# The field pairs of layer 0 in six tiles and a remainder of 35 pairs, instead of seven tiles

## What is computed

```python
x0 = xk = inputs                      # (512, 39, 16)
for idx, (W, b) in enumerate(params): # W: (39, fk, 128)
    z = jnp.einsum('bhd,bkd,hks->bsd', x0, xk, W) + b[None, :, None]
    z = jax.nn.relu(z)
    if idx != n_layers - 1:
        xk = z[:, :64, :]; direct.append(z[:, 64:, :])
    else:
        direct.append(z)
logit = jnp.sum(jnp.concatenate(direct, axis=1), axis=-1)
```

## Time and profile before

| | |
|---|---|
| time, median of 3 runs | 683.54 us (683.5 to 683.76) |
| the profiled execution's own time, span | 687.57 us, 685.8 us |
| busy: PE, DVE, POOL, ACT | 633.7 (92%), 587.2 (86%), 315.5 (46%), 252.4 us (37%) |
| L647, f32 matmuls of the whole groups | x928, 434.5 us busy |
| L637, L638, L639, split groups | x256 each, 143.5, 101.5, 101.2 us |
| L582 and L574, products | x253 and x128 |
| DMA | 129.97 MB, mean 190 GB/s |

### The profile page before, as it was taken

The page is one execution under the profiler, slowest core; times in us unless marked ns, Lnnn a source line. Parts: engine busy times, 40 slices in busy tenths (PEclk is TensorE's granted clock), DMA queues, the critical chain, the costliest instruction groups (busy, mean ns, idle before and its releaser), DMA issues.

```text
span 685.8 us, 5970 instructions
## 1 busy us (share of the span) xinstructions
PE 633.7 (92%) x1856; PEld 347.2 (51%) x1856; DVE 587.2 (86%) x548; ACT 252.4 (37%) x330; POOL 315.5 (46%) x391
## 2 busy tenths in 40 slices
PE   0169798979999999999999999999999999999998
PEld 0025354535555555555555555555555555555544
DVE  2049798968999999999999999999999999999920
ACT  2013335324434434343344443443434444333312
POOL 6752764746546453636464454635473131322210
PEclk9979999989999999999999999999999999999999
DMA  9689818864765849394857567584939474260100
GB/s 209 172 268 359 246 42 291 247 238 127 227 222 158 298 126 328 61 332 94 293 155 249 191 188 267 148 305 90 349 59 327 111 260 170 86 220 1 63 0 1
DMA packets 125630, 129.97 MB, mean 190 GB/s; under 512 B 59646, under 2 KB 67598, under 8 KB 125599
## 3 DMA queue, kind: packets, MB, share of 16 engines
q1 hardware_dynamic: 117679, 128.16, 57.6%
q0 software_dynamic: 5120, 1.32, 2.1%
q10 hardware_dynamic: 2800, 0.12, 0.3%
HBM read 123.18 MB, written 6.39 MB: 189 GB/s over the span
## 4 chain that ended last, share of the span: by engine, by line
PE 79%; ACT 0%; issue 0%
PE z L647 50%; PE z L637 8%; PE z L638 7%; PE z L639 7%; PE z L654 1%; PE z L711 1%; PE z L655 1%; PE top L701 1%; PE z L701 0%; PE tp L701 0%; PE top L694 0%; PE xk L717 0%; PE tp L628 0%; PE tp L630 0%; PE z L694 0%; PE tp L694 0%
## 5 line engine op out<-in xcount | busy, mean ns | idle before, releaser
L647 PE MATMUL z<-whole,w 128*128 128x512 f32 (+2 forms) x928 | 434.5, 601 | 17.0 <-DVE whole L582 16.2
L647 PEld LDWEIGHTS z<-whole,w 128*128 128x128 f32 (+2 forms) x928 | 177.5, 193 | 176.6 <-issue 156.7
L582 DVE TENSOR_TENSOR whole<-bc,xk 128x1024 f32<-128x1024 f32 (+1 forms) x208 | 231.3, 1131 | 28.6 <-PE z L647 19.5
L421 ACT ACTIVATE high<-raw 128x1024 fp32r<-128x1024 f32 (+1 forms) x128 | 135.3, 1058 | 293.4 <-DVE raw L574 238.6
L320 POOL DMA_INDIRECT emb<-in_tables,rows_all x160 | 169.7, 1060 | 54.4 <-issue 53.6
L558 DVE TENSOR_TENSOR low<-raw,high 128x1024 fp32r<-128x1024 f32 (+1 forms) x128 | 161.7, 1263 | 7.9 <-issue 4.6
L637 PE MATMUL z<-high,w_high 128*128 128x512 f32 (+1 forms) x256 | 143.5, 561 | 9.7 <-issue 5.6
L574 DVE TENSOR_TENSOR raw<-bc,xk 128x1024 f32<-128x1024 f32 x112 | 135.8, 1212 | 0.0
L338 POOL TENSOR_TENSOR stack<-stack_raw,stack 64x512 fp32r<-64x512 f32 x32 | 45.0, 1406 | 196.9 <-ACT stack L428 196.8
L638 PE MATMUL z<-high,w_low 128*128 128x512 f32 (+1 forms) x256 | 101.5, 397 | 0.0
L639 PE MATMUL z<-low,w_high 128*128 128x512 f32 (+1 forms) x256 | 101.2, 395 | 0.0
(11 more groups left out here) (55 smaller groups left out, 179.2 us busy)
## 6 DMA issues: line engine op xcount, KB each, us to landing
bc<-fields SPq DMA_DIRECT2D x64, 1024.0 KB, 5.9
rot<-fields SPq DMA_DIRECT2D x16, 1280.0 KB
bc<-fields SPq DMA_DIRECT2D x16, 768.0 KB
rot<-fields SPq DMA_DIRECT2D x16, 512.0 KB
fields<-xt SPq DMA_DIRECT2D x64, 80.0 KB
bc<-fields SPq DMA_DIRECT2D x32, 128.0 KB
rep<-fields SPq DMA_DIRECT2D x48, 80.0 KB
emb<-in_tables,rows_all POOLq DMA_INDIRECT x160
```

Source lines behind the costliest of these rows:

```text
L421: act.activation(high[0:m, k % PART_SLOTS], raw[0:m, k % RAW_SLOTS], ACT.Copy).then_inc(high_ready, 1)
L582: nc.vector.tensor_tensor(whole[0:rows, n % WHOLE_SLOTS, 0:len(tiles)], left, right, ALU.mult).then_inc(whole_ready, 1)
L647: ins = nc.tensor.matmul(z[layer][:, :], w[layer][0:m, WHOLE_AT[layer, t], :], whole[0:m, k % WHOLE_SLOTS, u], start=(t == 0), stop=(layer ...
```

## The change

Layer 0 has six tiles of 128 rows: `left0` now holds the fields in four runs with different rotations, chosen so that with the six right windows RIGHT0 the 768 rows meet 745 of the 780 pairs (a repeated pair has weight 0). The 35 pairs left over are loaded three times, into 105 rows of `rest`, left and right factor, with 12 DMAs. Their product goes through `stack_raw` and `stack`: ACT copies all 105 rows, rows 64 to 98 become the low part, and the weights (high or low per row, in an additional slot of `w_high`) are laid out so that one fp32r pass does what the split groups do in three. Layer 0 has three groups, the second split.

The low part is subtracted by the DVE for chunks 0 to 2 and by GpSimd from chunk 3 on, between the fold of layer 2 and the stack of (1, p + 1). The pass itself is put into the next step's groups: behind the second group for chunks 1 and 2, behind the eighth (g = 7, layer 1 of chunk c - 1) from chunk 3 on, and at the end of layer 0 in chunk 0. `layer0_out` waits for it. All stacks, those of layer 0 too, have numbers in STACK_NO. Weight preparation has a few more small operations. The diff, cut (slices of ROWS0 rows that become all 128 are left out, and so are the weight preparation and the host's layout):

```diff
-ROT = FIELDS // 2 + 1
-ROT_PER_TILE = PART // FIELDS
-T0 = -(-ROT // ROT_PER_TILE)
-TURN = FIELDS + 1
-ROWS0 = ROT_PER_TILE * TURN
-LAST0 = (ROT - (T0 - 1) * ROT_PER_TILE) * TURN
+RUNS0 = ((0, 6), (FIELDS, 10), (2 * FIELDS, 37), (3 * FIELDS, 0))
+RIGHT0 = (10, 11, 12, 13, 28, 29)
+T0 = len(RIGHT0)
+REST = ((11, 11, 17), (11, 10, 18))
+REST_ROWS = sum(length for _, _, length in REST)
+COPIES = 3
+REST_ALL = slice(0, COPIES * REST_ROWS)
+REST_LOW = slice(KEEP, KEEP + REST_ROWS)
...
+REST_BY_VECTOR = 3
+REST_AFTER = (1, 7)
...
+def left0_field(p):
+    return (p + [distance for first, distance in RUNS0 if first <= p][-1]) % FIELDS
...
-        STACK_NO = {x: n for n, x in enumerate(x for x in STEPS if x[0])}
+        STACK_NO = {x: n for n, x in enumerate(STEPS)}
+        REST_BEHIND = {STEPS[n + 1]: x[1] for n, x in enumerate(STEPS[:-1]) if x[0] == 0 and x[1]}
...
         def layer0_read(engine, c):
...
+            engine.wait_ge(stack_ready, STACK_NO[0, c] + 1)
+        def load_rest(queue, c):
+            for copy in range(COPIES):
+                row = copy * REST_ROWS
+                for field, distance, length in REST:
+                    for side, first in enumerate((field, field + distance)):
+                        src = bass.AP(fields.tensor, c * CHUNK_ROWS + first * N, [[N, length], [1, N]])
+                        queue.dma_start(rest[row:row + length, side, :], src).then_inc(rest_in, 16)
+                    row += length
...
-                for r in range(ROT_PER_TILE):
-                    src = bass.AP(fields.tensor, at, [[N, TURN], [1, N]])
-                    sp.dma_start(rep[r * TURN:(r + 1) * TURN, :], src).then_inc(rep_in, 16)
+                for (first, distance), (end, _) in zip(RUNS0, RUNS0[1:] + ((PART, 0),)):
+                    src = bass.AP(fields.tensor, at + (first + distance) % FIELDS * N, [[N, end - first], [1, N]])
+                    sp.dma_start(rep[first:end, :], src).then_inc(rep_in, 16)
                 if c > 1:
                     layer0_read(sp, c - 1)
-                for first, last, arrived in ((0, GT, rot_first), (GT, T0, rot_rest)):
-                    src = bass.AP(fields.tensor, at + first * ROT_PER_TILE * N, [[N, PART], [ROT_PER_TILE * N, last - first], [1, N]])
-                    sp.dma_start(rot[:, first:last, :], src).then_inc(arrived, 16)
+                for t in range(0, T0, GT):
+                    src = bass.AP(fields.tensor, at + RIGHT0[t] * N, [[N, PART], [(RIGHT0[t + 1] - RIGHT0[t]) * N, GT], [1, N]])
+                    sp.dma_start(rot[:, t:t + GT, :], src).then_inc(rot_rest if t else rot_first, 16)
+                if c:
+                    load_rest(sp, c)
...
             def stack_part(layer, c):
+                n, lower = STACK_NO[layer, c], slice(KEEP, PART) if layer else REST_LOW
                 own_done()
-                pool.wait_ge(stack_high, STACK_NO[layer, c] + 1)
-                pool.tensor_tensor(stack[KEEP:PART, :], stack_raw[KEEP:PART, :], stack[KEEP:PART, :], ALU.subtract).then_inc(stack_low, 1)
-                issued["stacks"] += 1
+                pool.wait_ge(stack_high, n + 1)
+                pool.tensor_tensor(stack[lower, :], stack_raw[lower, :], stack[lower, :], ALU.subtract).then_inc(stack_low, 1)
+                issued["stacks"] = n + 1
...
                 fold(2, p - 1)
+                if p + 2 in IN:
+                    stack_part(0, p + 2)
                 if p + 1 in IN:
                     stack_part(1, p + 1)
...
-                n = STACK_NO[layer, c]
+                n, filled = STACK_NO[layer, c], slice(0, PART) if layer else REST_ALL
                 act.wait_ge(stack_ready, n + 1)
                 if n:
                     act.wait_ge(stack_free, n)
-                act.activation(stack[:, :], stack_raw[:, :], ACT.Copy).then_inc(stack_high, 1)
+                act.activation(stack[filled, :], stack_raw[filled, :], ACT.Copy).then_inc(stack_high, 1)
...
-                act.wait_ge(whole_free, wholes_to(0, c, G0 - 1))
+                act.wait_ge(stack_free, STACK_NO[0, c] + 1)
...
+            act.wait_ge(stored, 16 * STORES)
+            load_rest(act, 0)
             for g in SPLIT[0]:
                 high_part(0, 0, g)
+            turned(1)
+            stack_part(0, 0)
             layer0_out(0)
...
             turned(2)
             for g in SPLIT[0]:
                 high_part(0, 1, g)
+            stack_part(0, 1)
             layer0_out(1)
...
                 layer2_out(p - 1)
+                if p + 2 in IN:
+                    stack_part(0, p + 2)
...
-                        dve.wait_ge(rot_rest, (c + 1) * 16)
+                        dve.wait_ge(rot_rest, (c + 1) * 16 * (G0 - 1))
                     tiles = tiles_of(0, g)
-                    m = LAST0 if T0 - 1 in tiles else ROWS0
-                    product(0, c, g, rot[0:m, tiles[0]:tiles[-1] + 1, :], left[0:m, None, :].to_broadcast([m, len(tiles), N]))
+                    product(0, c, g, rot[:, tiles[0]:tiles[-1] + 1, :], left[:, None, :].to_broadcast([PART, len(tiles), N]))
                     lows(LAG)
+                n = STACK_NO[0, c]
+                if n:
+                    dve.wait_ge(stack_low, n)
+                dve.wait_ge(rest_in, (c + 1) * 16 * COPIES * len(REST) * 2)
+                nc.vector.tensor_tensor(stack_raw[REST_ALL, :], rest[:, 0, :], rest[:, 1, :], ALU.mult).then_inc(stack_ready, 1)
+                lows(LAG)
+                if c == 0:
+                    rest_low(0)
+            def rest_low(c):
+                n = STACK_NO[0, c]
+                dve.wait_ge(stack_high, n + 1)
+                nc.vector.tensor_tensor(stack[REST_LOW, :], stack_raw[REST_LOW, :], stack[REST_LOW, :], ALU.subtract).then_inc(stack_low, 1)
...
+                    if g == 0 and (layer, c) in REST_BEHIND and REST_BEHIND[layer, c] < REST_BY_VECTOR:
+                        rest_low(REST_BEHIND[layer, c])
...
-                    m = LAST0 if layer == 0 and t == T0 - 1 else ROWS[layer]
-                    ins = nc.tensor.matmul(z[layer][:, :], w[layer][0:m, WHOLE_AT[layer, t], :], whole[0:m, k % WHOLE_SLOTS, u],
-                                           start=(t == 0), stop=(layer == 0 and t == T0 - 1))
+                    ins = nc.tensor.matmul(z[layer][:, :], w[layer][:, WHOLE_AT[layer, t], :], whole[:, k % WHOLE_SLOTS, u],
+                                           start=(t == 0), stop=False)
...
+            def rest_of(c):
+                pe.wait_ge(stack_low, STACK_NO[0, c] + 1)
+                nc.tensor.matmul(z[0][:, :], w_high[REST_ALL, PARTS, :], stack[REST_ALL, :], start=False, stop=True).then_inc(stack_free, 1)
...
+                    if (layer, c) in REST_BEHIND:
+                        other = REST_BEHIND[layer, c]
+                        if g == REST_AFTER[other >= REST_BY_VECTOR]:
+                            rest_of(other)
                 if layer:
                     stacked(layer, c)
+                elif c == 0:
+                    rest_of(0)
```

More of the change, by code:

```diff
@@ L85, in tower @@
         w = [sb(f"w{n}", [PART, W[n], OUT]) for n in range(3)]
[L86 to L87 removed]
+        w_high = sb("w_high", [PART, PARTS + 1, OUT], fp32r)
+        w_low = sb("w_low", [PART, PARTS + 1, OUT], fp32r)
         wt3 = sb("wt3", [PART, H2 // PART])
@@ L99, in tower @@
         rot = sb("rot", [PART, T0, N])
-        rep = sb("rep", [ROWS0, N])
+        rest = sb("rest", [COPIES * REST_ROWS, 2, N])
+        rep = sb("rep", [PART, N])
         bc = [sb(f"bc{n}", [PART, T1, N]) for n in range(2)]
@@ L118, in tower @@
         to_split = rows[:, 0:PARTS, :]
-        w0_rev = rows[:, PARTS:PARTS + T0, :]
+        w0_rev = rows[:, PARTS:PARTS + T0 + 2, :]
+        rest_w = rows[:, PARTS + T0 + 2:PARTS + T0 + 4, :]
         wt1 = bc[0][:, 0:2, :]
@@ L132, in tower @@
         top = [bank(f"top{n}") for n in range(2)]
-        left0 = top[1][0:ROWS0, :]
+        left0 = top[1][:, :]
         h1_banks = (top[0], top[1], tp, z[0])
@@ L416, in high_part @@
             def high_part(layer, c, g):
-                k, m = SPLIT_NO[layer, c, g], ROWS[layer]
+                k = SPLIT_NO[layer, c, g]
                 act.wait_ge(raw_ready, k + 1)
@@ L555, in low_part @@
             def low_part(layer, c, g):
-                k, m = SPLIT_NO[layer, c, g], ROWS[layer]
+                k = SPLIT_NO[layer, c, g]
                 dve.wait_ge(high_ready, k + 1)
-                nc.vector.tensor_tensor(low[0:m, k % PART_SLOTS], raw[0:m, k % RAW_SLOTS], high[0:m, k % PART_SLOTS], ALU.subtract).then_inc(low_ready, 1)
+                nc.vector.tensor_tensor(low[:, k % PART_SLOTS], raw[:, k % RAW_SLOTS], high[:, k % PART_SLOTS], ALU.subtract).then_inc(low_ready, 1)
             def lows(age):
@@ L567, in product @@
             def product(layer, c, g, left, right):
-                m = ROWS[layer]
                 if g in SPLIT[layer]:
@@ L580, in product @@
                     tiles = tiles_of(layer, g)
```

(36 more changed lines are left out.)

55 lines of the change are left out of this document (31 added, 24 removed).

## The result

The changed kernel takes **734.13 us** (median of 4 runs, 732.11 to 736.15) against 683.52 for the kernel before on the same chip: ratio **1.0727** (95% interval 1.0689 to 1.0765), 50.6 us slower. The forecast was 701.3 with a range up to 714. The time is close to the 736 of another rival, the landing in the burst; that is a coincidence, since the landing waits were 0.5 us a cycle longer than forecast and not 3.5.

What follows compares the result with a forecast made beforehand. TensorE was taken as the bound at 37.37 us a cycle, the DVE close behind. +4.4 through p = 1 (including +1.2 at the start), +14.6 for ten cycles, -1.1 and 0.1 at the end: +17.8, median 701.3, range 677 to 714.

Steps and rivals of the forecast that it cites:

- the landing in the burst: Rival: in the cycles, gathers land among the `rep` and `rot` loads, +3.5 for ten cycles, 736; chance 0.18, shared with very late rows.
- The bound: Steady cycle: TensorE never idles in 37.37 us, the DVE could do 36.4; after the change TensorE needs 36.6 without waits.
- the passes: TensorE, per chunk: one f32 tile (0.86) goes and one fp32r pass (0.233) comes, -0.62 a cycle.
- the products: DVE, per chunk: an 80x512 product goes and a 105x512 one comes, 0.60 either way, so 0.
- (a): Up to the third chunk: `z[0]` emptied later, TensorE's wait at (2, 0) about 4; net +1.2, between -1 and +5.
- (b): At p = 1: the DVE's product waits for the rest subtraction after a late landing; next stack product at 159.8, +4.4.
- a rival of their own: The 35 rows arrive late: 17-row loads use one engine, chunks 0 and 3 wait, +5, 706; much too late shares chance 0.18.
- the rule: Loads of the rest: a DMA uses the largest engine count up to 16 dividing its rows, so 17 rows use one.
- (c): Ten cycles with gathers, p = 2 to 11: the DVE waits on GpSimd, 39.0 a cycle against 37.37, +14.6.
- the fold's collision: End of GpSimd's chain: the fold falls into the DVE's third subtraction, begins at 20.44 and takes 2.0, to 22.44.
- (d): p = 12 and 13, a rest but no gathers: TensorE bounds, 36.9 and 36.75 against 37.37 twice, -1.1.
- The rival of the Trainium skill's SBUF page: GpSimd's gathers start on time despite DVE subtractions, the DVE hardly waits, cycles about 36.85 to 36.9, 679.6; chance 0.20.

Runs made afterwards that it cites:

- the last version: The changed kernel with 18-row pieces, a separate stack for the rest, and ACT serving layer 2's first split group before emptying `z[0]` of chunk 1: 676.17 us, ratio 0.9905.
- with full loads: The changed kernel with all pieces of the rest at 18 rows instead of 17 and 18, its wait on GpSimd kept: 714.09 us, ratio 1.0445.

## Why the prediction missed

**The bound, the passes, the products: right.** TensorE's 36.6 us a cycle were an inference from start-to-start times; the last version runs at it. The DVE's subtractions of layer 1 stood where the forecast had laid them: at 12.53, 15.93 and 19.33 in the cycle shown.

**(a) and (b), the start: wrong, by 20.4 of 24.8 us.** The forecast was 159.8 for the first stack product of layer 2 behind p = 1; 180.20 was measured. The step that failed is the place of the rest's DMAs in the sum. It stood there as twelve issues on SP at 0 cost, with the data spread over 16 engines, 1.3 us; the loads through one engine were put in a rival of their own, whose price was +5, in chunks 0 and 3 only. The runs show 22.6 us in four chunks, and 20.0 or 23.9 for the pieces of 17 rows alone. Two things went wrong in it. I took the steady cycle's slack of 20 us as the rule and looked at the start for two chunks, though in chunks 2 and 3 the last of the twelve loads is issued (106.45 and 136.63) only 2.7 and 2.1 us before the DVE wants the rows (109.18 and 138.71). In chunks 0 and 1 the DVE wants them 10.1 and 7.9 us behind the last issue, about the 9.1 that the slow loads alone take, and waits 6.24 and 2.54; other transfers ran beside them there, at 258 to 377 GB/s from 30 to 40 us, and what part of the wait is theirs was not separated. And I gave the rule little because no row bore it out, where no row spoke against it either. The other half of (a) was right: the wait at (2, 0) forecast at about 4 was 4.60,

```profile
93.91 0.79 PE L701 MATMUL z<-high,w_high 128*128 128x512 f32 x1 [4.60 <-DVE low L610]
```

and with full loads the start came 0.8 us from the forecast.

**(c), the ten cycles: right in kind, too small by 8 of 22.6 us.** The DVE waits for GpSimd in ten cycles, as forecast, but 3.4 us each. The cycle was 39.83 and not 39.0; the mis-sized term is the chain of GpSimd, 24.68 on average and not 23.85, by the second gather (2.56 or 2.57 in each of the ten cycles and not 1.43) and the landing (2.03 on average and not 1.51), less the fold's collision that did not come (0.96 in the cycle shown). Taking the landing "as today" was a choice that no row bore out for a chain that ends later in the cycle. The forecast's own range for this term, up to 39.5 a cycle, was too narrow.

**(d), the tail: right in kind.** -2.9 where the steps gave -1.1 and -0.1; the two cycles without gathers took 35.83 and 36.62.

**The rival of the Trainium skill's SBUF page** ("SBUF — State Buffer", "Who interferes with whom"), GpSimd in time at 679.6, fell with the gathers: at 264.56, 272.42 and 275.47 they were held by the DVE's operations with two SBUF inputs, each to 0.82 behind the end of such an operation. What this refutes is the rival and not cleanly the section's inference: the gathers here are indirect and read their row numbers (`rows_all`) from SBUF, and by the same section GpSimd's reads do contend. No run has a DMA of GpSimd without such a read. In the kernel with a stack of its own the gathers are held as long (2.57 at 270.03), and it costs nothing: no wait of TensorE or the DVE for GpSimd shows in its cycle.

**What stays open.** Why landing waits vary from 1.48 to 3.25 from cycle to cycle was not tried. Nor was it why the second gather is held through two DVE operations, while the one at 8.96 in the kernel before, and one at 8.97 in the changed kernel (1.43 us), fit the end of the first of several in a row. It is also open what part of the fall in the granted clock (0.967 for the changed kernel, 0.992 for the best) is a cost by itself and what part only goes with TensorE's waits.

## What to carry to other kernels

A saving on the bound engine is worth nothing while a new hand-over ties that engine's supplier to a slow chain: here 0.6 us a cycle of TensorE were paid with 2.5 us a cycle, and a buffer of 2 KB, with the orders that it made possible, undid that. Before a helper engine is given a job whose result a busy engine waits for, lay out its whole chain and ask what else could wait instead; the job was harmless once its own buffer let it slide into idle time. And do not put a load's price by its bytes alone: with the same number of loads and 3% more bytes, 18 rows for 17, by one row of weight zero, were worth 20 us.

## What the runs showed of the hardware

- Loads of 17 and of 19 rows of 2 KB moved at 23 to 25 GB/s where nothing but gathers ran beside them, the broadcasts of 128 rows in the same view at up to 391. In the first view 5.7% of 16 engines' time went into them, nine tenths of one engine. Six such loads of 17 rows a chunk cost 20 to 24 us; twelve of 19 cost 170 (854.68, one run, against 684.58), of which 151.3 are the DVE's waits for the rows. The broadcasts issued behind them landed after 16.4 us instead of 7.6.
- A GpSimd gather that begins under two DVE operations with two SBUF inputs that follow each other without a gap was held through both in each of the ten steady cycles of the two kernels (2.56 us at 264.56 in the changed kernel, 2.57 at 270.03 in the best version). This is no general rule: the gathers at 8.96 and 8.97 named above were released after the first.
- Gathers whose last packets are issued as a burst of loads begins landed after 5.39 us (4.02 to 5.93 over ten cycles) instead of 1.51.
